# A four-layer kernel on one core: its convolution kernel made in two halves of 16 heads, the second behind the second strip group, and fewer weight levels within the convolution

## The reference

```python
x = x + ffn0(cond0(x, lengths, log_dt, C, log_A_real, A_imag, D))   # fp8 weight, 512x512
x = x + ffn1(cond1(x, adapter_ids))                                 # 16 adapters; NF4 weights, hidden 1376
x = x + ffn2(cond2(x, language_ids))                                # LoRA experts; router over 128 slots
x = x + ffn3(cond3(x, lengths))                                     # gated mean; LoRA mixture
```

```python
dtA = (-exp(log_A_real) + 1j * A_imag) * exp(log_dt)[:, None]
Cs = C * (exp(dtA) - 1) / A
K = 2 * einsum('hn,hnl->hl', Cs, exp(dtA[:, :, None] * arange(512))).real   # h = 32 heads, n = 64 modes
y = causal_conv(u * mask, K) + u * mask * D[:, None];  y = y * mask
```

## Time and profile before

| | |
|---|---|
| three runs | 957.39, 950.3, 953.33 us; median 953.33 |
| the profiled execution | 951.24 us, span 949.5 us |
| TensorE busy | 885.1 us (93% of the span) |
| VectorE busy | 579.8 us (61%) |
| ScalarE busy | 390.1 us (41%) |
| GpSimd busy | 86.9 us (9%) |
| granted TensorE clock, mean | 0.992 |
| read from HBM | 51.07 MB |

### The profile page before, as it was taken

How to read it: one execution, slowest core, us unless ns; L and a number is a source line. 1 busy time by engine, 2 the same in 40 slices (tenths; PEclk the granted TensorE clock), 3 DMA queues, 4 the chain that set the end, 5 groups by cost and what they waited for, 6 DMA issues and landing times.

```text
span 949.5 us, 10316 instructions
## 1 busy us (share of the span) xinstructions
PE 885.1 (93%) x3261; PEld 474.5 (50%) x3262; DVE 579.8 (61%) x880; ACT 390.1 (41%) x458; POOL 86.9 (9%) x127
## 2 busy tenths in 40 slices
PE   0299998999999999999999999999989999899998
PEld 0296448998444444444444444444434555354442
DVE  7889977886998888888997300000132354158444
ACT  2024637876777776676687100000012132241200
POOL 5100009600000000000000000002201011100000
PEclk9999998999999999999999999999999999999999
DMA  6873127562000000000000300024010000002022
GB/s 203 317 242 134 74 81 246 195 223 70 23 22 23 17 31 0 31 30 1 30 1 0 87 13 1 0 72 136 1 45 1 1 1 1 1 1 44 0 89 88
DMA packets 32967, 61.19 MB, mean 64 GB/s; under 512 B 5880, under 2 KB 8264, under 8 KB 31704
## 3 DMA queue, kind: packets, MB, share of 16 engines
q1 hardware_dynamic: 32216, 60.50, 18.8%
q0 software_dynamic: 704, 0.10, 0.3%
HBM read 51.07 MB, written 8.47 MB: 63 GB/s over the span
## 4 chain that ended last, share of the span: by engine, by line
PE 83%; DVE 12%; issue 2%; DMA 1%; ACT 1%; POOLq 1%; POOL 0%; SPq 0%; ACTq 0%; DVEq 0%
PE ps L820 81%; DVE acc L1374 2%; DVE T L1374 2%; PE ps L861 1%; DVE W2T L1218 1%; PE ps L1075 1%; DVE W2T L1224 1%; POOLq L603 1%; DVE W2T L1221 1%; DVE raw L1352 0%; DVE amax L1345 0%; DMA T<-kpad 0%; DVE W1T L1218 0%; DVE Up L1551 0%; DVE Yp L1659 0%
## 5 line engine op out<-in xcount | busy, mean ns | idle before, releaser
L652 ACT ACTIVATE above<-raw,cst 128x1024 bf16<-128x1024 f32 (+2 forms) x225 | 271.8, 1231 | 122.1 <-DVE acc L1374 46.5
L820 PE MATMUL ps<-Yp,W3T 128*128 (+2 forms) x872 | 183.9, 367 | 6.6 <-POOL Yp L605 2.6
L1374 DVE SCALAR_TENSOR_TENSOR acc<-above,acc 128x1024 f32<-128x1024 bf16 (+2 forms) x112 | 148.1, 1323 | 18.3 <-ACT above L652 11.6
L820 PE MATMUL ps<-Up,W1T 128*128 128x512 f32 x344 | 155.5, 594 | 3.0 <-DVE Up L1473 1.9
L820 PE MATMUL ps<-Up,W2T 128*128 128x512 f32 (+1 forms) x392 | 155.1, 593 | 0.0
L820 PEld LDWEIGHTS ps<-Yp,W3T 128*128 128x128 f32 (+1 forms) x872 | 121.9, 196 | 63.7 <-issue 61.5
L1374 DVE SCALAR_TENSOR_TENSOR T<-above,T 128x1024 f32<-128x1024 bf16 (+1 forms) x84 | 114.1, 1359 | 20.9 <-ACT above L652 18.0
L820 PE MATMUL ps<-X,W3T 128*128 128x512 f32 (+1 forms) x256 | 113.7, 602 | 0.6 <-DVE Yp L1659 0.6
L820 PEld LDWEIGHTS ps<-Up,W2T 128*128 128x128 f32 (+1 forms) x392 | 64.2, 177 | 83.0 <-issue 83.0
L820 PEld LDWEIGHTS ps<-Up,W1T 128*128 128x128 f32 x344 | 64.1, 190 | 82.5 <-issue 76.3
L1495 DVE TENSOR_TENSOR X<-X,Yp x16 | 4.6, 349 | 125.6 <-issue 125.6
(11 more groups left out here) (299 smaller groups left out, 753.4 us busy)
## 6 DMA issues: line engine op xcount, KB each, us to landing
W3T<-in_wa SPq DMA_DIRECT2D x11, 1024.0 KB, 6.3
raw<-in_w SPq DMA_DIRECT2D x20, 256.0 KB, 3.3
W3T<-kpad SPq DMA_DIRECT2D x9, 512.0 KB, 5.0
Up<-in_xconv SPq DMA_DIRECT2D x4, 1024.0 KB, 11.5
X<-in_xT SPq DMA_DIRECT2D x1, 4096.0 KB, 22.9
xkeep<-X SPq DMA_DIRECT2D x4, 1024.0 KB, 4.5
X<-xkeep SPq DMA_DIRECT2D x4, 1024.0 KB, 9.6
W3T<-in_wa SPq DMA_DIRECT2D x5, 768.0 KB, 4.6
```

What stands on the lines that cost most here:

```text
L652: nc.scalar.activation(above[0:h, m % 2, 0:w], raw[0:h, u % 2, 0:w], ACT.Relu, scale=STEEP, bias=cst[0:h, C_BND + i:C_BND + i + 1]).then_i ...
L820: return nc.tensor.matmul(o, l, r, start=start, stop=stop, **kw)
L1374: V.scalar_tensor_tensor(out=ac, in0=src, scalar=float(STEPS[i]), in1=ac, op0=ALU.min, op1=ALU.add).then_inc(s["m_used"], 1)
```

## The change

K is made in two halves: heads 0 to 15 (f = 0) and 16 to 31 (f = 1). Angles, whole turns, Sin, factors, products (banks 6 and 7), the addition of D and the stores to `kpad` are each done twice on half of the heads. Within a half the four row blocks hold HE = 4 heads each, so D is loaded in another order. The second half's products stand on TensorE behind group 1, and its stores on SP behind strip 4. The fp8 weight's dequantising is moved on VectorE behind the masking of group 3, and load_unit(1) on SP from behind strip 4 to behind strip 8. X is loaded in four transfers of 1 MB, two where it was and two behind strips 8 and 12. The convolution has four levels of the NF4 weights in place of 10, the fp8 layer 28 in place of 26, and the adapters 54 in place of 50. The list of semaphores, which gains l_kq0 to l_kq3, is left out of the diff.

```diff
         n0 += 2 * S * LA
-        HQ = S // 4
+        HQ, HF, HE = S // 4, S // 2, S // 8
         ksb = w2f[:, n0:n0 + HQ * LC].rearrange("p (h m) -> p h m", h=HQ)
...
         PARTS = LEV * NU
-        NCV, NF0, NAD = 10, 26, 50
+        NCV, NF0, NAD = 4, 28, 54
         UP_A, UP_B = 21, 21
...
             for q in range(4):
-                sp.dma_start(sm[q * 32:q * 32 + 1, 5, 0:HQ], A["Dskip"][q * HQ:(q + 1) * HQ].rearrange("(a h) -> a h", a=1)
-                             ).then_inc(s["l_dsk"], 16)
+                sp.dma_start(sm[q * 32:q * 32 + 1, 5, 0:HQ].rearrange("p (f i) -> p f i", f=2),
+                             A["Dskip"].rearrange("(a f q i) -> a q f i", a=1, f=2, q=4)[:, q]).then_inc(s["l_dsk"], 16)
             for c in range(DC):
...
+            def load_x(c):
+                sp.dma_start(X[:, c, :], A["xT"][c * P:(c + 1) * P, :]).then_inc(s["l_x"], 16)
             load_unit(0)
-            sp.dma_start(X[:, :, :], A["xT"].rearrange("(c p) n -> p c n", p=P)).then_inc(s["l_x"], 16)
+            load_x(0)
+            load_x(1)
...
             kr = kv[:, PAD:KROW].rearrange("h (a c) -> a h c", a=LA)
-            sp.wait_ge(s["d_k"], 1)
-            for q in range(4):
-                sp.dma_start(kr[:, q * HQ:(q + 1) * HQ, :], ksb[q * 32:q * 32 + LA, :, :]).then_inc(s[f"l_kp{q}"], 16)
+            def store_k(f):
+                sp.wait_ge(s["d_k"], f + 1)
+                for q in range(4):
+                    h = f * HF + q * HE
+                    sp.dma_start(kr[:, h:h + HE, :], ksb[q * 32:q * 32 + LA, f * HE:(f + 1) * HE, :]).then_inc(s[f"l_k{'pq'[f]}{q}"], 16)
+            store_k(0)
             sp.wait_ge(s["l_kpz"], 16)
...
                     sp.wait_ge(s[f"l_strip{g % NS}"], 16 * (g // NS))
-                if g * GH % HQ == 0:
-                    sp.wait_ge(s[f"l_kp{g * GH // HQ}"], 16)
+                if g * GH % HE == 0:
+                    sp.wait_ge(s[f"l_k{'pq'[g * GH // HF]}{g * GH // HE % 4}"], 16)
                 sp.dma_start(strips[g % NS], bass.AP(kpad, g * GH * KROW + 1, [[1, P], [KROW, GH], [1, D]])
...
                 if g == NS - 1:
+                    store_k(1)
+                if g == HG // 2:
                     sp.wait_ge(s["d_w0"], 1)
...
+                if g in (8, 12):
+                    load_x((8, 12).index(g) + 2)
                 for u in units_between(K_CONV[g - NS - 1] if g > NS else 0, K_CONV[g - NS]) if g >= NS else []:
...
             nc.scalar.activation(sm[:, 12, :], sm[:, 8, :], ACT.Sin, scale=turn1 / 2).then_inc(s["a_ang"], 1)
-            act.wait_ge(s["d_ang"], 2)
-            nc.scalar.activation(trig, whole, ACT.Sin, scale=-turn1).then_inc(s["a_ang"], 1)
+            for f in range(2):
+                hs = slice(f * HF, (f + 1) * HF)
+                act.wait_ge(s["d_ang"], f + 2)
+                nc.scalar.activation(trig[:, hs, :], whole[:, hs, :], ACT.Sin, scale=-turn1).then_inc(s["a_ang"], 1)
...
-            pe.wait_ge(s["d_pp"], 1)
-            pe.wait_ge(s["d_kz"], 1)
-            for i in range(HQ):
-                for q in range(4):
-                    h = q * HQ + i
-                    last = mm(ps[q * 32:q * 32 + LA, 6, i * LC:(i + 1) * LC], pc[:, h, :], trig[:, h, 0:LC], True, True)
-            last.then_inc(s["p_k"], 1)
+            pe.wait_ge(s["d_kz"], 2)
+            def make_k(f):
+                pe.wait_ge(s["d_pp"], f + 1)
+                for i in range(HE):
+                    for q in range(4):
+                        h = f * HF + q * HE + i
+                        last = mm(ps[q * 32:q * 32 + LA, 6 + f, i * LC:(i + 1) * LC], pc[:, h, :], trig[:, h, 0:LC], True, True)
+                last.then_inc(s["p_k"], 1)
+            make_k(0)
             pe.wait_ge(s["l_cst"], 16)
...
                     elif n + m < 2:
-                        pe.wait_ge(s["d_k"], 1)
+                        pe.wait_ge(s["d_k"], 2)
                     else:
...
                 last.then_inc(s["p_conv"], 1)
+                if g == 1:
+                    make_k(1)
...
             V.memset(zpad, 0.0).then_inc(s["d_zp0"], 1)
-            V.memset(ps[:, 6, 0:HQ * LC], 0.0).then_inc(s["d_kz"], 1)
+            for f in range(2):
+                V.memset(ps[:, 6 + f, 0:HE * LC], 0.0).then_inc(s["d_kz"], 1)
...
             V.tensor_tensor(dec, a_.unsqueeze(2).to_broadcast([P, S, CMULT]), mul, ALU.mult).then_inc(s["d_ang"], 1)
-            tt(trig[:, :, 0:CMULT], f_.unsqueeze(2).to_broadcast([P, S, CMULT]), mul, ALU.mult)
-            ts(trig[:, :, CMULT:], trig[:, :, LC:CMULT], 0.25, None, ALU.add, ALU.bypass)
-            ts(trig[0:MODES, :, 0:LC], trig[0:MODES, :, 0:LC], 0.25, None, ALU.add, ALU.bypass)
-            ts(whole, trig, ROUND, None, ALU.add, ALU.bypass)
-            V.scalar_tensor_tensor(out=whole, in0=whole, scalar=ROUND, in1=trig, op0=ALU.subtract, op1=ALU.subtract
-                                   ).then_inc(s["d_ang"], 1)
+            def angles(f):
+                hs = slice(f * HF, (f + 1) * HF)
+                tt(trig[:, hs, 0:CMULT], f_[:, hs].unsqueeze(2).to_broadcast([P, HF, CMULT]), mul[:, hs, :], ALU.mult)
+            def whole_turns(f):
+                hs = slice(f * HF, (f + 1) * HF)
+                ts(trig[:, hs, CMULT:], trig[:, hs, LC:CMULT], 0.25, None, ALU.add, ALU.bypass)
+                ts(trig[0:MODES, hs, 0:LC], trig[0:MODES, hs, 0:LC], 0.25, None, ALU.add, ALU.bypass)
+                ts(whole[:, hs, :], trig[:, hs, :], ROUND, None, ALU.add, ALU.bypass)
+                V.scalar_tensor_tensor(out=whole[:, hs, :], in0=whole[:, hs, :], scalar=ROUND, in1=trig[:, hs, :],
+                                       op0=ALU.subtract, op1=ALU.subtract).then_inc(s["d_ang"], 1)
+            angles(0)
+            whole_turns(0)
             expm1(a_, sl_[18], True, [sl_[19], sl_[20], sl_[21], sl_[22]])
...
             ts(be[hi], cr[hi], -2.0, None, ALU.mult, ALU.bypass)
-            dve.wait_ge(s["a_ang"], 5)
-            tt(trig[:, :, 0:LC], trig[:, :, 0:LC], dec[:, :, 0:LC], ALU.mult)
-            tt(pc, trig[:, :, CMULT:], al.unsqueeze(2).to_broadcast([P, S, LA]), ALU.mult)
-            tt(pq, trig[:, :, LC:CMULT], be.unsqueeze(2).to_broadcast([P, S, LA]), ALU.mult)
-            tt(pc, pc, pq, ALU.add)
-            V.tensor_tensor(pc, pc, dec[:, :, LC:], ALU.mult).then_inc(s["d_pp"], 1)
-            dve.wait_ge(s["p_k"], 1)
-            dve.wait_ge(s["g_dsk"], 3)
-            V.tensor_tensor(ksb, ps[:, 6, 0:HQ * LC].rearrange("p (h c) -> p h c", c=LC), kdk, ALU.add).then_inc(s["d_k"], 1)
+            def factors(f):
+                hs = slice(f * HF, (f + 1) * HF)
+                dve.wait_ge(s["a_ang"], 5 + f)
+                tt(trig[:, hs, 0:LC], trig[:, hs, 0:LC], dec[:, hs, 0:LC], ALU.mult)
+                tt(pc[:, hs, :], trig[:, hs, CMULT:], al[:, hs].unsqueeze(2).to_broadcast([P, HF, LA]), ALU.mult)
+                tt(pq[:, hs, :], trig[:, hs, LC:CMULT], be[:, hs].unsqueeze(2).to_broadcast([P, HF, LA]), ALU.mult)
+                tt(pc[:, hs, :], pc[:, hs, :], pq[:, hs, :], ALU.add)
+                V.tensor_tensor(pc[:, hs, :], pc[:, hs, :], dec[:, hs, LC:], ALU.mult).then_inc(s["d_pp"], 1)
+            def skip_term(f):
+                o = slice(f * HE, (f + 1) * HE)
+                dve.wait_ge(s["p_k"], f + 1)
+                dve.wait_ge(s["g_dsk"], 3)
+                V.tensor_tensor(ksb[:, o, :], ps[:, 6 + f, 0:HE * LC].rearrange("p (h c) -> p h c", c=LC), kdk[:, o, :], ALU.add
+                                ).then_inc(s["d_k"], 1)
+            factors(0)
+            angles(1)
+            skip_term(0)
+            whole_turns(1)
...
                             ).then_inc(s["d_oneh"], 1)
+            factors(1)
...
                         dve.wait_ge(s[f"l_kp{q}"], 16)
+                        dve.wait_ge(s[f"l_kq{q}"], 16)
                 if i == 0 and banks_before(u):
...
             start_unit(0)
-            dve.wait_ge(s["l_w0"], 32)
-            link(V.tensor_copy(h16a, w0u))
-            link(V.tensor_scalar(h16b, h16a, 0x7F, 7, ALU.bitwise_and, ALU.logical_shift_left))
-            link(V.tensor_scalar(h16a, h16a, 0x80, 8, ALU.bitwise_and, ALU.logical_shift_left))
-            link(V.tensor_tensor(h16a, h16a, h16b, ALU.bitwise_or))
-            V.tensor_scalar(w0, h16a.bitcast(f16), 256.0, None, ALU.mult).then_inc(s["d_w0"], 1)
+            skip_term(1)
             dve.wait_ge(s["p_ord"], 1)
...
                 link(V.tensor_scalar(mnat[:, c, :], lenf[:, 0, :], cst[:, C_L + c:C_L + c + 1], None, ALU.is_gt))
+            def dequantise_w0():
+                dve.wait_ge(s["l_w0"], 32)
+                link(V.tensor_copy(h16a, w0u))
+                link(V.tensor_scalar(h16b, h16a, 0x7F, 7, ALU.bitwise_and, ALU.logical_shift_left))
+                link(V.tensor_scalar(h16a, h16a, 0x80, 8, ALU.bitwise_and, ALU.logical_shift_left))
+                link(V.tensor_tensor(h16a, h16a, h16b, ALU.bitwise_or))
```

(6 more changed lines are left out.)

2 lines of the change are left out of this document (1 added, 1 removed).

## The result

The changed kernel took 965.79 us (median of 4, 964.57 to 967.31), the kernel before 955.36 us in the same session (950.3 to 957.64). The ratio is 1.0124, 95% interval 1.0094 to 1.0153. The profiled execution took 965.71 with a span of 963.9 (before 951.24 and 949.5), so the two spans differ by 14.4 us, of which about 4 is the draw of the kernel before, whose profiled execution was near its fastest. The prediction had 957.7 and a range up to 963: too low. I go through the profile after in the order in which the prediction went.

A forecast was written before the change was run, and what follows sets the result against it. TensorE was taken as the bound, with 83% of the chain. Terms -4.9 + 0.55 + 7.4 + 1.85 - 0.5 gave +4.4 us on the median 953.3: 957.7 us, range 951 to 963 (8 in 10).

The forecast's parts named there:

- The first half earlier: Start of the convolution: with K halved, TensorE's first strip product comes at 37.3 instead of 42.24, 4.9 us earlier.
- Products inside the convolution: TensorE makes the second half's products behind groups 0 and 1, adding 0.55 us to the convolution.
- The five dequantising instructions: VectorE's later dequantising of the fp8 weights takes 5.1 us without GpSimd interfering, so d_w0 comes at 60.7.
- Strip 9 waits: In the convolution, strip 9 queues behind the d_w0 wait and lands at 68.9; TensorE, ready at 61.5, waits 7.4 us.
- The restart: After the idle at strip 9 TensorE runs at half clock, costing 1.85 us (0 to 1.9).
- Masking: End of the convolution: one masking instead of two stands behind the last group, saving 0.5 us.
- The moved levels in the fp8 layer: 28 levels instead of 26 give VectorE 2.5 us more work in the fp8 layer; counted as 0.
- The moved levels in the adapter stage: 54 levels instead of 50 and unit 3's start make ScalarE late; counted as 0, up to 3.7 us.
- My second rival: Over 1% slower: the strip 9 wait plus a second TensorE wait in the adapter stage; +9.8, 963.1 us, chance 0.12.

The follow-up runs named there:

- e1: Changed kernel with SyncE's wait for d_w0 and unit 1's load moved behind the last strip: 953.35 us, ratio 1.0008 to the kernel before.
- e9: Changed kernel with unit 1's load and the third piece of X behind strip 9, the d_w0 wait still ahead of it: 964.67 us.
- e10: e7 with level plan 4, 32, 50 (convolution, fp8 layer, adapters) in place of 4, 28, 54: 951.77 us, ratio 0.9994 to the kernel before.
- e2: Changed kernel with the old level plan 10, 26, 50 in place of 4, 28, 54: 958.62 us, ratio 1.0068 to the kernel before.
- e3: Kernel before with the new level plan 4, 28, 54 alone, without the halves: 957.19 us, ratio 1.0043 to the kernel before.
- e7: e1 with unit 3's raw load issued ahead of adapter 2 and the last save of X: 953.62 us, ratio 0.9998 to the kernel before.
- e8: e1 with 50 levels in the adapter stage instead of 54, four more in the gated layer: 956.58 us, ratio 1.0023 to the kernel before.
- e12: The same kernel as e7, unchanged, run again for a second profile: 950.83 us, ratio 0.9979 to the kernel before.
- e4: Changed kernel with dequantising before the second skip term, unit 1's load behind strip 4, old levels 10, 26, 50: 953.08 us, ratio 0.9987 to the kernel before.
- e13: Kernel before, unchanged, run again for a second profile: 952.5 us, against 952.56 for the kernel before in that session.
- e6: e4 with unit 1's load moved from behind strip 4 to behind strip 8: 953.55 us, ratio 0.9999 to the kernel before.

## Why the prediction was wrong, point by point

**The first half earlier, -4.9:** right. Measured -4.7 (37.56 for 37.3), and 37.1 to 37.7 in all ten experiments with the halves. The first d_k came at 30.52 for the 30.5 predicted, the first strip's issue at 33.40 for 32.9.

**Products inside the convolution, +0.55:** 0.43 measured. But groups 0 and 1 took 7.48, start to start, for the 6.70 counted (45.04 less 37.56), and with the start 0.3 later d_w0 came at 61.52 for 60.7. This is the chance named above; in e1 it came at 60.15.

**The five dequantising instructions, 5.1:** 5.2 (56.34 to 61.52), the second at 0.69. The Trainium skill, "SBUF — State Buffer", section "Who interferes with whom", has the exclusion of VectorE and GpSimd that I leaned on; the trace agrees, with 0.69 where GpSimd idles for 2.27 where it worked. GpSimd lost too, which I did not count: its normalising took 2.93 us beside the cast in the kernel before, and 1.90 alone in the changed one (at 39.70).

**Strip 9 waits, +7.4:** the mechanism was right and e1 and e9 show it. The size was 0.8 low: issue at 62.95 for 62.2, landing after 7.8 from its own issue, at 70.7 for 68.9. I had placed the landing 8.2 us after d_w0, between two bounds; it was 9.2, near the upper one (9.6).

**The restart, +1.85:** mis-sized. 3.1 us after the idle of 8.17. The row that I took it from was the start of the convolution, where the idle before was 4.16 and groups 0 and 1 lose 1.9 us; with the halves that row itself moves by 1.4 us from execution to execution, and the range (0 to 1.9) had no room for more.

**Masking, -0.5:** right in itself (1.11 for 1.60). The sum to the fp8 layer was +4.4 and came out at +7.5.

**The moved levels in the fp8 layer, 0:** right for 28 levels. e10 shows how near the edge that is.

**The moved levels in the adapter stage, "So 0, and up to 3.7":** this is the step that failed. It cost 6.5 us in the profiled execution (4.8 and a restart of 1.7), and 7.2 by e2's median, more than the end that I allowed. I took the 5.38 us of VectorE's wait further on for slack that absorbs what comes before it, and looked for ScalarE's lag in the middle of the stage; TensorE lost at its start, through adapter 3 (which I did not follow at all, though its issue stands behind the raw load in the same queue), and at its end. e3 shows it without the halves (+3.9), e7 and e8 its two parts. My second rival had this and gave 963.1; it had the raw load as the cause, which is half of it, and a chance of 0.12 that was too small.

**The numbers.** By spans the sum had +4.4 and should have had 7.5 + 4.8 + 1.7 = +14.0. The range's upper end stopped at 963 although its own two upper bounds, 7.5 at the convolution and 3.7 in the adapter stage, give 964.5 together; they were not added. Even 964.5 is below the median measured.

## What to carry to other kernels

A queue that waits holds everything behind it: for each load that a change moves, follow the next loads in the same queue to their landings, not only the engine that wants the moved one. An engine that gains a head start gives it back at the next engine that is full in that stage (here VectorE in the convolution), so count that engine's work from its first possible start to the stage's end before crediting the gain. And work moved out of a stage must be costed in the stage where it lands: here two levels more or less in one stage (28, 30, 32) decided between no loss, 1 us and 7.

## What the runs showed of the hardware

The half clock behind an idle of TensorE is no fixed price. Behind 8.17 us it read 0.50 for 6 us and cost 3.1. Behind 3.8 to 4.8 us it cost between 1.6 (9.68 for 8.05 in after and e1) and 2.8 (10.86 for 8.05 behind 4.33 in e3). Behind 2.1 to 3.0 us it cost about 1.7 in most rows (5.40 for 3.70 in after, e1, e9 and e12; 6.70 for 4.98 in e4), and nothing in one (32 matmuls in 3.81 behind 2.15, e9 at 151.95). Behind 1.9 to 2.0 us either: 1.7 behind 1.88 in e8, 1.6 behind 1.98 in e12, nothing behind 2.02 in e7, and behind 1.97 both, in two executions of one kernel (e7 and e12, and the kernel before and e13). Behind 1.59 and 1.60 us nothing (e3, and the fp8 layer). So a few idles of some 2 us make a kernel's executions differ by as much as the change under study, and a single profile can lie several us from the median: e7's was 4.3 below it.

A strip of 512 KB took 4.3 us to land from its own issue with no load just ahead (e9), 6.1 behind two loads of 256 KB (e4), and 7.8 behind these and 1 MB (after). What was issued behind it differed too, so the three are not a rule for adding up loads.

A GpSimd instruction and VectorE's cast and tensor_scalar over 2048 columns held each other up: 2.93 us for 1.90 on GpSimd, 2.27 for 0.69 on VectorE (the kernel before, e3, e4, e6 and e13, against the kernels with the later dequantising).
